# Moving the transposition of a head's maxima from the third to the fifth unit, and the output bias from head 1 to heads 14 and 15

## What is computed

```python
q = (hidden_states @ q_w.T + q_b).reshape(b, s, H, HEAD_DIM)
k = hidden_states @ k_w.T + k_b
v = hidden_states @ v_w.T + v_b
scores = jnp.einsum('bqhd,bkd->bhqk', q, k) / HEAD_DIM ** 0.5
scores = jnp.where(causal[None, None], -jnp.inf, scores)
attn = jax.nn.softmax(scores.astype(jnp.float32), axis=-1)
out = jnp.einsum('bhqk,bkd->bqhd', attn, v).reshape(b, s, H * HEAD_DIM)
return out @ o_w.T + o_b
```

## Time and profile before

| | |
|---|---|
| time, median of 3 runs | 2046.67 us (2044.64 to 2047.15) |
| profiled execution, its own time | 2041.99 us |
| its span | 2040.3 us |
| PE busy in the span | 1979.5 us (97%) |
| DVE busy | 1187.8 us (58%) |
| ACT busy | 794.9 us (39%) |
| idle time of PE before L1332 and L1478 | 14.0 and 4.4 us |

### The profile page before, as it was taken

The page is one execution under the profiler, slowest core; times in us unless marked ns, Lnnn a source line. Parts: engine busy times, 40 slices in busy tenths (PEclk is TensorE's granted clock), DMA queues, the critical chain, the costliest instruction groups (busy, mean ns, idle before and its releaser), DMA issues.

```text
span 2040.3 us, 26384 instructions
## 1 busy us (share of the span) xinstructions
PE 1979.5 (97%) x9120; PEld 1459.5 (72%) x9120; DVE 1187.8 (58%) x2603; ACT 794.9 (39%) x1337; POOL 150.2 (7%) x522
## 2 busy tenths in 40 slices
PE   7999999999999999899999999999999999999998
PEld 3456666666666556556888888888888888888887
DVE  6687776677767555676455455444554455445433
ACT  3366555555556553465221322222222223232121
POOL 0111111112111111112000000000000000000000
PEclk9999999999999999999999999999999999999999
DMA  7443344334443455645335334344343353443431
GB/s 226 122 109 75 97 114 110 93 90 103 108 113 70 140 162 167 204 134 192 134 134 193 126 125 167 124 131 165 124 165 124 124 170 120 157 141 124 154 124 62
DMA packets 113659, 271.43 MB, mean 133 GB/s; under 512 B 27754, under 2 KB 33130, under 8 KB 113400
## 3 DMA queue, kind: packets, MB, share of 16 engines
q1 hardware_dynamic: 104168, 248.71, 40.1%
q10 hardware_dynamic: 9360, 21.04, 3.1%
HBM read 194.96 MB, written 31.74 MB: 111 GB/s over the span
## 4 chain that ended last, share of the span: by engine, by line
PE 53%; DVE 1%; DMA 1%; ACT 0%; SPq 0%; issue 0%; POOL 0%; POOLq 0%; DVEq 0%; ACTq 0%
PE banks L1277 34%; PE banks L1433 17%; PE banks L1375 1%; PE banks L1369 1%; DMA upgate_raw<-in_w_ug 0%; PE banks L1501 0%; DMA inverse_sums_dram<-sums 0%; DVE out_sb L1050 0%; DVE out_sb L1041 0%; ACT probs L783 0%; DMA o_group<-o_raw 0%; PE banks L1345 0%; ACT h_crossed_split L699 0%; SPq L426 0%; POOL probs L856 0%
## 5 line engine op out<-in xcount | busy, mean ns | idle before, releaser
L1277 PE MATMUL banks<-h_t_split,w_ring 128*128 128x512 f32 x3072 | 717.4, 389 | 0.6 <-DVE w_ring L1015 0.6
L1277 PEld LDWEIGHTS banks<-h_t_split,w_ring 128*128 128x128 f32 x3072 | 576.4, 188 | 120.8 <-DVE w_ring L1015 1.0
L716 ACT ACTIVATE silu_gate<-banks,scale_upgate 128x512 f32<-128x512 f32 x128 | 88.2, 689 | 800.7 <-PE banks L1277 800.7
L1433 PE MATMUL banks<-d_ring,y_split 128*128 128x512 f32 x1536 | 370.5, 390 | 0.1
L1023 DVE SCALAR_TENSOR_TENSOR y<-banks,scale_upgate,silu_gate 128x512 f32<-128x512 f32 x128 | 96.0, 750 | 433.3 <-ACT silu_gate L716 433.3
L783 ACT ACTIVATE probs<-banks 128x512 f32<-128x512 f32 x576 | 312.5, 601 | 58.3 <-PE banks L1478 52.2
L1433 PEld LDWEIGHTS banks<-d_ring,y_split 128*128 128x128 f32 x1536 | 287.2, 188 | 59.6 <-DVE y_split L1029 0.5
L1501 PE MATMUL banks<-probs,v_ones 128*64 128x512 f32 (+3 forms) x1536 | 279.5, 499 | 3.0 <-POOL probs L856 3.0
L1332 PE MATMUL banks<-k_stack,q_stacks 96*128 96x512 f32 (+3 forms) x768 | 248.5, 366 | 14.0 <-ACT neg_max_rows L637 5.7
L1478 PE MATMUL banks<-q_stacks,k_stack 98*128 98x512 f32 (+3 forms) x768 | 249.9, 367 | 4.4 <-ACT probs L783 4.3
L1501 PEld LDWEIGHTS banks<-probs,v_ones 128*64 128x64 f32 x1536 | 118.4, 137 | 163.4 <-issue 136.0
(11 more groups left out here) (123 smaller groups left out, 1249.4 us busy)
## 6 DMA issues: line engine op xcount, KB each, us to landing
upgate_raw<-in_w_ug SPq DMA_DIRECT2D x128, 512.0 KB, 4.3
d_ring<-down_split_dram SPq DMA_DIRECT2D x128, 512.0 KB, 3.3
q_stacks<-q_split SPq DMA_DIRECT2D x192, 128.0 KB, 2.4
o_group<-o_raw SPq DMA_DIRECT2D x128, 128.0 KB, 2.3
x<-in_x SPq DMA_DIRECT2D x32, 256.0 KB, 3.1
o_group<-inverse_sums_dram SPq DMA_DIRECT2D x64, 128.0 KB, 2.8
x_and_residual<-in_x SPq DMA_DIRECT2D x32, 256.0 KB, 4.5
x_dram<-x_and_residual SPq DMA_DIRECT2D x32, 256.0 KB, 2.5
```

Of the source, the lines that this page charges most:

```text
L1277: ins = nc.tensor.matmul(out, weights(a, k), moving(m, k), start=(k == 0 and a + m == 0), stop=(last and k == kts - 1 and a == 1))
L1433: last = nc.tensor.matmul(acc[:, t, :], ys[s][:, a, t * P:(t + 1) * P], dr[g % D_RING][:, m, :], start=(f == 0 and a + m == 0), stop=(f == ...
```

## The change

`top` moves from unit 2 to unit 4 and there stands behind `max` 4 instead of ahead of the unit's `max`. The three instructions of the bias move from the start of head 1 to unit 4 of heads 14 (two) and 15 (one).

```diff
-TOP_UNIT, FIRST_WEIGHED = 2, 6
+TOP_UNIT, FIRST_WEIGHED = 4, 6
-PROJECTION_STEPS = (1, 5)
+PROJECTION_STEPS, BIAS_STEP = (1, 5), 14
@@ side_work
-    if 0 < H < heads - 1:
-        units[TOP_UNIT].append(("top", H + 1))
     if 0 < H < heads - AHEAD:
         for i in range(NS):
             units[i].append(("max", H + AHEAD, i))
+    if 0 < H < heads - 1:
+        units[TOP_UNIT].append(("top", H + 1))
@@ vector engine, step
-                if H == PROJECTION_STEPS[0]:
-                    projection_bias()
@@
-            def projection_bias():
-                dve.wait_ge(ob_in, 32)
-                dve.wait_ge(const_ready, 2)
-                nc.vector.tensor_copy(ob[0:1, :], ob_raw[0:1, :])
-                chain.link(nc.vector.tensor_copy(ob[2 * HD:2 * HD + 1, :], ob_raw[2 * HD:2 * HD + 1, :]))
-                chain.link(nc.vector.tensor_tensor(ob[2 * HD:2 * HD + 1, :], ob_raw[2 * HD:2 * HD + 1, :],
-                                                   ob[2 * HD:2 * HD + 1, :].bitcast(F32), ALU.subtract))
+            def projection_bias(part):
+
+                if part == 0:
+                    dve.wait_ge(ob_in, 32)
+                    dve.wait_ge(const_ready, 2)
+                    nc.vector.tensor_copy(ob[0:1, :], ob_raw[0:1, :])
+                    chain.link(nc.vector.tensor_copy(ob[2 * HD:2 * HD + 1, :], ob_raw[2 * HD:2 * HD + 1, :]))
+                else:
+                    chain.link(nc.vector.tensor_tensor(ob[2 * HD:2 * HD + 1, :], ob_raw[2 * HD:2 * HD + 1, :],
+                                                       ob[2 * HD:2 * HD + 1, :].bitcast(F32), ALU.subtract))
@@ prepare
+                if H >= BIAS_STEP and H - BIAS_STEP < 2 and u == PART_ENDS[0]:
+                    projection_bias(H - BIAS_STEP)
```

## The result

The changed kernel takes 2062.07 us (median of 6 runs, 2057.97 to 2064.11); the kernel before, run beside it, 2044.68 us (2041.70 to 2047.15). The ratio is 1.0084, with a 95% interval of 1.0073 to 1.0095: 17 us slower, where 19.7 was worked out. The profiled execution of after has a span of 2061.1 us against 2040.3.

What follows compares the result with a forecast made beforehand. In attention DVE's freeing of three side banks paces a head's first half, PE the second. Terms by class sum to +19.7 us, taking the profiled 2041.99 to 2061.7, or the median 2046.67 to 2066.3, forecast as 2066, range 2057 to 2076.

Steps and rivals of the forecast that it cites:

- What bounds the kernel: Attention: DVE's freeing of three side banks paces a head's first half, PE alone the second; PE busy 855 of 894 us.
- The two prices: Before the first value products: 0.15 us from reduction's end to transposition, 0.20 from transposition to value products.
- DVE's reductions keep their times.: First half of a head: reductions stand in line from max 0 on, and max 0 doesn't move.
- reductions that move with the change: Profile of attention: a named sign that the prediction is wrong; no size given.
- the 1.2 that was named: Heads with `out`: PE sits idle about 1.2 us ahead of the transposition, a named sign of being right.
- The cover of 0.05 for the score of unit 8: Second half: ACT's 0.27 later probabilities still come 0.05 us ahead of this score; without cover, up to 0.27 a head.
- the bank that max 6 takes too early: Second half, where rows or a fold stand behind: 0.2 us a head, mostly disappearing; heads 12, 28, 44 together +0.6.
- The gather: On SP behind the small DMA: moves 0.8 us later, but its readers come late enough; no loss counted.
- The small DMA: Between heads: issued about 3.5 us ahead, took 2.55, covered by 1 us; lateness as a rival +16, 2082, chance 0.03.
- the faster case: First halves: DVE's release of max 2 is not late, so PE runs through; 2026 to 2031, chance 0.06.
- The stall: Second halves held by DVE or ACT would absorb a later first half: no change, 2047, chance 0.04.
- The clock: New waits in 32 attention heads drop PE to half clock; one in three losing 1 us: +11, 2077, chance 0.07.

Runs made afterwards that it cites:

- bias_only: The kernel before with only the three bias instructions moved to heads 14 and 15; 2046.47 us beside 2043.99 of before, ratio 1.0009.
- unit2_behind: The changed kernel with the transposition back in unit 2, but behind that unit's max; 2054.57 us, ratio to before 1.0047.
- experiment 7: The changed kernel with SP issuing the gather of the value products ahead of the small DMA of the maxima; 2081.38 us, ratio to before 1.0177.
- experiments 5 and 6: The kernel before and the changed kernel, each with every unmasked reduction over half its columns; 2035.65 and 2036.40 us.
- top_only: The kernel before with only the transposition moved to unit 4 behind max 4, the bias left in head 1; 2061.81 us, ratio 1.0084.
- gather_first: The kernel of experiment 7: the changed kernel with the gather issued ahead of the small DMA on SP; 2081.38 us, ratio to before 1.0177.
- half_before: The kernel before with every unmasked reduction over half of its columns only; 2035.65 us, ratio to before 0.9950.
- half_after: The changed kernel with every unmasked reduction over half of its columns only; 2036.40 us, ratio to before 0.9957.
- top_behind_values: The changed kernel with the transposition in unit 5 ahead of max 5, behind the first value products; 2029.82 us, ratio to before 0.9929.

## Why the prediction was right, point by point

**What bounds the kernel.** Right. The first half of a head is paced by DVE's freeing of banks, the second by PE. Halving the reductions takes the change's loss from 17 to 0.75 us, and a piece moved into the second half costs its own 0.12 there or more.

**The two prices.** Release to transposition 0.15 is what head 34 shows (513.30 to 513.45), and transposition to value products 0.20 in plain and `out` heads (513.45 to 513.65, 568.89 to 569.09). Both were taken between bounds, and no bound was needed.

**"DVE's reductions keep their times."** This is the step that failed, by 0.07 to 0.1 us a head. It was argued with "they stand in line behind each other from max 0 on, and max 0 doesn't move". But two reductions in line can overlap by 0.09 if the second one's product is there in time. In a plain head of before it wasn't: the product of max 2 stood behind the transposition on PE and, by the modelled ends of the trace, landed 2.04 us into the head, just when DVE came to it; in after it lands at 1.74, and DVE starts at 2.00 instead of 2.07. `bias_only` and `unit2_behind` test it: they differ in nothing but whether the transposition stands ahead of max 2 or behind it, in the same unit. In the first the reduction of max 2 in head 34 (starts at 502.28) ends at 505.04 and so begins at 504.35, 2.07 in; in the second (head 34 starts at 504.96) it begins 2.00 in:

```profile
503.67 1.37 DVE L880 TENSOR_REDUCE max_all<-banks 128x1 f32<-128x512 f32 x2
...
506.96 0.68 DVE L880 TENSOR_REDUCE max_all<-banks 128x1 f32<-128x512 f32 x1
```

The first row is `bias_only`, the second `unit2_behind`. So the plain heads came out at -0.02 instead of +0.08, `rows` at +0.50 instead of +0.57, folds at +0.51 instead of +0.57, `kv` (first halves) at -0.37 instead of -0.27. In `out` heads, where DVE's own two instructions for `out` set the time, nothing could move: +0.71 against +0.72. Over the plain, `rows`, fold and `kv` heads that is about 17 x 0.10 + 9 x 0.07 + 7 x 0.06 + 3 x 0.10 = 3.1 of the 3.2 us between 19.7 and 16.5. The prediction named reductions that move with the change as a sign of being wrong, and this one came, in this small size. The other misses are as large but cancel: head 5 (+0.86), heads 54 to 56 (+0.5), 49 and 61 (-0.3), 6 and 7 (-0.6), 1 to 3 (-2.2, most of it the clock of head 1), 46 (+1.0, the clock again), 57 to 63 (+0.4). That they cancel is luck. The idle time ahead of the transposition in heads with `out` was 0.92 by the profile, not the 1.2 that was named.

**Second half.** The cover of 0.05 for the score of unit 8 held: plain heads lost nothing there (-0.04 to +0.03). Where the prediction has 0.2 for the bank that max 6 takes too early, heads 12, 28 and 44 show +0.20 to +0.21 at the score of unit 8 (0.17 at the start of the next head), and 54 to 56 show +0.22 to +0.24 as well, which were left out. Heads 6 and 7 lost 0.14 there instead of 0.27 and gained 0.45 ahead of it instead of 0.3.

**The gather.** "Its readers come heads later or behind ACT's query copies" was wrong in one head. In head 5 the reader comes before the split of the queries, 0.86 us, and experiment 7 gave it back.

**The small DMA.** "Covered by 1 us" was 1.6 us: the 2.55 of the earlier trace rows is longer than the 2.00 of head 34 in experiment 7. No first score product of after waits for it.

**The rivals.** The release is late, so the faster case is out; experiments 5 and 6 show that it needs DVE's reductions at half length to be even. The stall is not absorbed. The clock: this rival was rarer than its one head in three, not absent. The new waits are of 0.92 us in 12 heads and of 1.52 in three, not of 0.9 to 1.4 in 32. The eight heads with `out` between 326 and 610 us of after have the 0.92 and a granted clock of 1.00 throughout. Behind the 1.52 of head 11 the clock fell in `top_only` and cost 1.7 us, and in `gather_first` it fell behind that of head 43 (654.0 us); in the profiled execution of after it fell behind none of the three, which is luck, and how often it does in the runs that were only timed isn't known. Head 46 speaks neither for nor against: its wait for probabilities is 1.46 in after and 1.16 in before, but `bias_only` and `half_before` have a low stretch there with the 1.16. The Trainium skill (TensorE: Matmul & The Clock Gate, Why this matters for your kernels) says that an idle gap between bursts of matmuls, if it is long enough, sends PE back to half rate. The traces here show the fall behind gaps, but not each time: behind the 1.52 us of head 11 in `top_only`, and not behind the same gap in after.

**The basis.** The forecast added 4.7 us since the profiled execution lay below the median of 3 runs. With 6 runs the median of before is 2044.68. On that basis 19.7 gives 2064.4, and 2062.07 was measured. So of the 4 us between it and the 2066 of the forecast (range 2057 to 2076) about half is the basis and half the size of the change.

## What to carry to other kernels

In a ring of three banks each piece waits for the release of the piece three places before it. So a move of one piece changes what the others wait for, even if the number of pieces ahead of a barrier stays the same, as here. Follow the list up to the barrier and read when the latest of these releases comes: before, the transposition stood where its bank, freed early by ACT, went to the last piece; in `unit2_behind` and after, the last piece waited for a reduction one later, and that cost 10 and 17 us. Put a short piece where the ring has slack, here behind the value products, and charge it there at its full length at least if PE paces that stretch. When a wait on one engine is taken away, ask next whether the engine behind it was waiting for the moved piece too: here a reduction of DVE moved by 0.07 us, because PE delivered its product sooner.

## What the runs showed of the hardware

The stretches at the lower clock move between traces. There were three in attention in before, after, `bias_only` and `half_after`, four in `top_behind_values` and `half_before`, five in `top_only` and `unit2_behind` and six in `gather_first`, and those that can be compared head by head are worth about 1 to 2 us each. `bias_only`, with three small instructions moved, has none in head 1 and one in head 46 (677.3 us). A wait of the same length is followed by one in some traces and not in others: 1.16 us in head 46 (not in before, but in `bias_only` and `half_before`), 1.52 in head 11 (in `top_only`, not in after). A single head's time in one profile can differ by 1 to 2 us for that reason alone. The time ahead of head 0 differed between profiled executions too, 57.4 to 62.0 us, with nothing changed there. Both are as large as the effects of whole classes here, so starts were compared head by head and summed by class.
